# A hybrid transformer on one Trainium2 core: the decayed q and k operands of the decay attention stay in PSUM until their first rest is taken

## What is computed

```python
q = x @ W_q
k = x @ W_k
v = x @ W_v
latent_kv = (k + v) @ W_down_kv
k_rec = (latent_kv @ W_up_k)          # per head of 8
v_rec = (latent_kv @ W_up_v)
scores = einsum('bhqd,bhkd->bhqk', q, k_rec) / sqrt(d)
decay = exp(-0.01 * abs(t[:, None] - t[None, :]))
attn = softmax(scores * decay)
out = einsum('bhqk,bhkd->bhqd', attn, v_rec)
```

## Time and profile before

| | us |
|---|---|
| median of 3 runs | 1121.29 |
| lowest, highest | 1120.91, 1122.62 |
| profiled execution, its own time | 1125.32 |
| its span in the trace | 1123.5 |
| TensorE busy (share of the span) | 1041.1 (93%) |
| VectorE busy | 743.8 (66%) |
| ScalarE busy | 678.7 (60%) |
| GpSimd busy | 170.5 (15%) |

### The profile page before, as it was taken

How to read it: one execution, slowest core, us unless ns; L and a number is a source line. 1 busy time by engine, 2 the same in 40 slices (tenths; PEclk the granted TensorE clock), 3 DMA queues, 4 the chain that set the end, 5 groups by cost and what they waited for, 6 DMA issues and landing times.

```text
span 1123.5 us, 15969 instructions
## 1 busy us (share of the span) xinstructions
PE 1041.1 (93%) x6036; PEld 413.5 (37%) x6048; DVE 743.8 (66%) x1194; ACT 678.7 (60%) x1140; POOL 170.5 (15%) x119
## 2 busy tenths in 40 slices
PE   5799998988999999999999989999989988999998
PEld 2233333335433333333333334443333333334443
DVE  2787326348989999999999621126879898881110
ACT  4687525446078788888888774467556656634331
POOL 0222531006000000000000000000333342340000
PEclk9899999999989999999999999999989999999999
DMA  8000000038950321303000000000000000000000
GB/s 270 1 2 1 1 0 1 0 123 233 303 90 4 64 43 23 65 4 63 9 3 8 7 2 1 1 1 0 1 0 1 0 1 0 1 10 1 10 9 10
DMA packets 31203, 38.37 MB, mean 34 GB/s; under 512 B 7964, under 2 KB 22300, under 8 KB 30744
## 3 DMA queue, kind: packets, MB, share of 16 engines
q1 hardware_dynamic: 31128, 37.37, 13.2%
HBM read 23.23 MB, written 13.86 MB: 33 GB/s over the span
## 4 chain that ended last, share of the span: by engine, by line
PE 51%; DVE 23%; ACT 6%; issue 2%; another core or an unknown queue 1%; DVEq 0%; ACTq 0%
PE PS L1510 17%; DVE ffn L926 15%; PE PS L1038 6%; PE PS L1014 4%; DVE PS L1063 2%; PE PS L1495 2%; PE PS L1498 2%; PE PS L1521 2%; ACT arena L1048 2%; PE PS L1577 1%; PE PS L1080 1%; PE PS L1687 1%; PE PS L916 1%; DVE arena L1724 1%; PE PS L1677 1%
## 5 line engine op out<-in xcount | busy, mean ns | idle before, releaser
L1048 ACT ACTIVATE arena<-PS 128x384 f32<-128x384 f32 (+1 forms) x512 | 258.0, 547 | 84.4 <-PE PS L1014 72.9
L926 DVE CUSTOM_DVE_ANT_0 ffn<-PS,XP 128x1024 bf16<-128x1024 f32 x256 | 300.7, 1216 | 4.4 <-PE PS L916 4.4
L916 PE MATMUL PS<-arena 48*128 48x512 bf16 (+3 forms) x704 | 173.6, 325 | 5.6 <-DVE MX L926 5.5
L1014 PE MATMUL PS<-arena 50*128 50x512 bf16 (+3 forms) x640 | 169.4, 320 | 1.6 <-ACT arena L1048 1.3
L1038 PE MATMUL PS<-arena 128*32 128x256 f32 x2048 | 162.4, 393 | 1.0
L1540 ACT ACTIVATE arena<-PS,w_scl 128x512 f32<-128x512 f32 x64 | 43.5, 687 | 139.5 <-PE PS L1510 139.2
L1510 PE MATMUL PS<-arena,w_h2T 128*128 128x512 f32 x256 | 118.0, 607 | 0.0
L1510 PE MATMUL PS<-arena,w_h1T 128*128 128x512 f32 x256 | 115.3, 594 | 0.4 <-DVE arena L1549 0.4
L1014 PEld LDWEIGHTS PS<-arena 50*128 50x128 bf16 x640 | 50.4, 94 | 101.9 <-ACT arena L1048 70.2
L1724 DVE TENSOR_TENSOR_SCAN arena<-arena 128x512 f32<-128x512 f32 x64 | 81.4, 1273 | 0.3
L1510 PEld LDWEIGHTS PS<-arena,w_h2T 128*128 128x128 f32 x256 | 49.6, 195 | 61.1 <-issue 58.6
(11 more groups left out here) (228 smaller groups left out, 1558.0 us busy)
## 6 DMA issues: line engine op xcount, KB each, us to landing
arena<-scr SPq DMA_DIRECT2D x64, 192.0 KB, 5.7
scr<-arena SPq DMA_DIRECT2D x16, 384.0 KB, 5.5
scr<-arena SPq DMA_DIRECT2D x16, 256.0 KB, 4.9
scr<-arena SPq DMA_DIRECT2D x16, 128.0 KB, 3.3
XP<-xT SPq DMA_DIRECT2D x1, 1024.0 KB, 4.9
w_h1T<-h1T SPq DMA_DIRECT2D x1, 1024.0 KB, 6.7
w_h2T<-h2T SPq DMA_DIRECT2D x1, 1024.0 KB, 8.6
arena<-MH SPq DMA_DIRECT2D x64, 4.0 KB, 1.7
```

The lines of the kernel that those rows point to most:

```text
L916: mm = t.matmul(PS[:, bank, k0 - lo:k1 - lo], packed(m, g, v, slice(q * P, (q + 1) * P), KP), packed(m, g, 2 + v, slice(k0, k1), KP), star ...
L926: v.tensor_tensor_reduce(JUNK[:, u % 2, :], PS[:, bank:bank + 2, :].rearrange("p a b -> p (a b)"), STRIP[:, at:at + S], 1.0, -3.0e38, ALU. ...
L1014: mm = t.matmul(PS[:, score_bank(T, i), at:at + b_ - a_], packed(n, g, 2 + v, slice(kt * P, (kt + 1) * P), KP + MROWS), packed(n, g, v, sl ...
L1048: nc.scalar.activation(PT[:, T % 2, score_head(T, i), a0_:a1_], PS[:, score_bank(T, i), a0_:a1_], ACT.Exp).then_inc(s_free, 1)
```

## The change

The four decayed operands are no longer written to SBUF but to PSUM: operand 0 to bank 5, operand 1 back into bank 0, operand 2 to bank 6 and operand 3 back into bank 3. ScalarE casts the high piece from there, and VectorE's subtraction reads the operand from PSUM and the high piece from SBUF; only the first rest is written to `V32`. VectorE takes rests 0 and 1 ahead of the copy of v, and rests 2 and 3 behind it. The wait for the low piece of two chunks earlier moves from the multiplication to the subtraction, since that is now what overwrites `V32`. TensorE's projections of the next chunk wait for the first rests 0 and 1 of the chunk before (`a1_r1`, at 4c - 2), the rebuilt k for all four of them, and the attention's first unit for all sixteen.

```diff
@@ -761,13 +761,15 @@
             return T % 2 == 0
 
 
+        DECAYED = (5, 0, 6, 3)
+
         def a1_prep_pe(t):
             wait_loads(t, 3)
             for c in range(NCH):
                 x = XN[:, c * CH:(c + 1) * CH]
                 t.wait_ge(ln_free, ln_count(4, c))
                 if c > 0:
-                    t.wait_ge(a1_ver, 4 * c - 2)
+                    t.wait_ge(a1_r1, 4 * c - 2)
                 t.matmul(PS[:, 0, :], wqkv1[:, 0:P], x, start=True, stop=True)
                 t.matmul(PS[:, 1, :], wqkv1[:, P:2 * P], x, start=True, stop=False)
                 t.matmul(PS[:, 1, :], wqkv1[:, 2 * P:3 * P], x, start=False, stop=True).then_inc(a1_qkv, 1)
@@ -778,6 +780,8 @@
                 t.wait_ge(a1_latc, c + 1)
                 t.wait_ge(ln_free, ln_count(4, NCH - 1))
                 t.wait_ge(a1_v, c + 1)
+                if c > 0:
+                    t.wait_ge(a1_r1, 4 * c)
                 t.matmul(PS[:, 3, :], wlow[:, P:2 * P], LAT, start=True, stop=True)
                 for w in range(CH // P):
                     mm = t.matmul(PS[:, 4, w * P:(w + 1) * P], LAT[:, w * P:(w + 1) * P], wlow[:, 2 * P:3 * P],
@@ -802,7 +806,7 @@
                     a.wait_ge(a1_stored[c % 2], STORES)
                 for v in range(4):
                     a.wait_ge(a1_ver, 4 * c + v + 1)
-                    nc.scalar.copy(SPL[c % 2][:, v, 0, :], V32[c % 2][:, v, :]).then_inc(a1_hi, 1)
+                    nc.scalar.copy(SPL[c % 2][:, v, 0, :], PS[:, DECAYED[v], :]).then_inc(a1_hi, 1)
                 if c + 1 < NCH:
                     take_kv(c + 1)
                     take_latent(c + 1)
@@ -822,16 +826,21 @@
                     c = b * 2 + j
                     v.wait_ge(a1_qkv, c + 1)
                     for n, tab in ((0, FALL), (1, RISE), (2, RISE), (3, FALL)):
-                        v.wait_ge(a1_lo_free, 4 * c + n + 1)
                         if n == 2:
                             v.wait_ge(a1_kr, c + 1)
-                        v.scalar_tensor_tensor(out=V32[j][:, n, :], in0=PS[:, 0 if n < 2 else 3, :],
+                        v.scalar_tensor_tensor(out=PS[:, DECAYED[n], :], in0=PS[:, 0 if n < 2 else 3, :],
                                                scalar=SCALE if n < 2 else 1.0, in1=tab[:, j * CH:(j + 1) * CH],
                                                op0=ALU.mult, op1=ALU.mult).then_inc(a1_ver, 1)
+
+                    def rest(n):
+                        v.wait_ge(a1_hi, 4 * c + n + 1)
+                        v.wait_ge(a1_lo_free, 4 * c + n + 1)
+                        v.tensor_tensor(V32[j][:, n, :], PS[:, DECAYED[n], :], SPL[j][:, n, 0, :], ALU.subtract).then_inc(a1_r1, 1)
+                    rest(0)
+                    rest(1)
                     v.tensor_copy(XN[:, chunk(c)], PS[:, 4, :]).then_inc(a1_v, 1)
-                    for n in range(4):
-                        v.wait_ge(a1_hi, 4 * c + n + 1)
-                        v.tensor_tensor(V32[j][:, n, :], V32[j][:, n, :], SPL[j][:, n, 0, :], ALU.subtract).then_inc(a1_r1, 1)
+                    rest(2)
+                    rest(3)
 
         def a1_minus_ones(g):
 
@@ -1120,6 +1129,7 @@
             a1_prep_pe(t)
             idle_pe(t, 18, 7)
             t.wait_ge(a1_v, 1 + NCH)
+            t.wait_ge(a1_r1, 4 * NCH)
             for u in range(LEAD):
                 unit_pe(t, u, 0)
                 unit_pe(t, u, 1)
```

## The result

The changed kernel is slower. Its median over 8 runs is 1135.18 us (1131.75 to 1138.98), against 1122.3 us (1120.72 to 1128.14) for 8 runs of the kernel before; the medians lie 12.9 us apart. The ratio on record is 1.0096, 95% interval 1.0075 to 1.0116, which is 10.8 us, from 8.4 to 13.0. The profiled execution took 1135.8 us with a span of 1134.0, against 1125.32 and 1123.5: 10.5 us in either. The prediction had +10.1 us, and a median of 1131.4 in a range of 1128.0 to 1135.0.

A forecast was written before the change was run, and what follows sets the result against it. The prediction took a TensorE and ScalarE chain to bound the preparation, with VectorE off it. Three borders of 2.80 us (8.4) plus 1.7 for the clock gave +10.1 on 1121.3: 1131.4 us, range 1128.0 to 1135.0.

The forecast's parts named there:

- The path: Preparation: TensorE and ScalarE alone form the chain, 7.07 us a chunk; the new wait adds VectorE, 8.4 us over three borders.
- The term of 2.80 us a border: Next chunk's q projection: starts near 251.22 instead of 248.42, waiting for multiplications 2 and 3 and rests 0 and 1.
- Rests ready when VectorE reaches them: ScalarE's casts of the high pieces finish before rests 0 and 1 need them, margin 0.9 us; cost 0.
- Hidden parts: Rebuilt k's wait for rest 3, `packs(0)` moving at most 5.6 us, and VectorE's own end add nothing.
- Cost of PSUM operands: Multiplications writing PSUM and subtractions reading it: 0.4 us of VectorE time, under 0.1 us on the path.
- The gain of 3 to 4 us of VectorE time: Subtractions beside GpSimd's should always take about 0.69 us, saving 3 to 4 us of VectorE's busy time, worth 0.
- The clock: Idle gaps of about 2.7 us at borders trip TensorE's clock to 0.50 once, 1.7 us; bounds 0 to 5.2.
- rival C: Attention: the later start moves the clock dip at 312 to 319 us away, returning up to 1.4 us; 1128.3 us, chance 0.09.
- The sum: Whole kernel: 8.4 for the waits + 1.7 for the clock = 10.1 us slower, median 1131.4 us.

The follow-up runs named there:

- e1: The change with decayed operand 1 in bank 7, so the q projection waits for the first two multiplications as before: 1122.11 us, ratio 1.000 to the kernel before.
- e2: The kernel before, operands in SBUF, with rests 0 and 1 ahead of the copy of v and the new projection wait: 1140.57 us, ratio 1.0153.
- e5: The change with rests 0 and 1 ahead of multiplications 2 and 3 in VectorE's order: 1130.25 us, ratio 1.0081 to the kernel before.
- e4: The change with 9 instead of 18 idle matmuls behind the last chunk: 1132.94 us, ratio 1.0085 to the kernel before.
- e3: The change with five idle matmuls behind the rebuilt v of chunks 0 to 2: 1128.78 us, ratio 1.0055 to the kernel before.
- e7: The changed kernel itself run once more, for a second profile: 1131.11 us, ratio 1.0085 to the kernel before.
- e6: As e5, with ScalarE casting high pieces 0 and 1 of chunks 1 and 2 right behind their latent: 1123.93 us, ratio 1.0025 to the kernel before.

## Why the prediction was right, point by point

*The path.* That the chain of before never touches VectorE in this stretch, and that the new wait puts it in, was the right reading; e1 and e2 separate the wait from the memory. The term of 2.80 us a border was 0.1 us too small: 9.97 - 7.07 = 2.90 between the later borders. From the end of the rebuilt v to the projection it is 251.53 - 248.89 = 2.64 us, just the predicted figure, but by two errors that cancel: the multiplication starts 0.02 us behind the rebuilt v, put at 0.11, and TensorE starts 0.14 us behind rest 1, put at 0.05. What was too small is the lost overlap of one matmul with the next: the first projection holds the chain for 1.10 us where it held it for 0.86, 0.24 us instead of the 0.16 in the sum.

*Rests ready when VectorE reaches them.* Right: in the change VectorE waits for TensorE and never for a cast at this point. The theory of e5, that ScalarE is next once the order is turned, held.

*Hidden parts.* The rebuilt k's wait for rest 3, the DMA queue, VectorE's own end: none shows in the profile after. `packs(0)` went from 270.41 to 275.10, 4.7 us, under the 5.6 that were its bound, and did not bind in e4. The bound counted two borders; the 4.7 us are one border of 2.90, the low stretch of 1.49 and the 0.29 from before it.

*Cost of PSUM operands.* Put at under 0.1 us. The rests show none, 678 ns against 678; the multiplications into PSUM have a mean of 694 ns where those into SBUF had 681, which for the six on the path is 0.08 us. The gain of 3 to 4 us of VectorE time without a gain in time was right too. What the prediction did not see is that in the new order these would have been on the path: e2 shows that with both inputs in SBUF borders 2 and 3 hold TensorE 1.5 us longer each. Next to e2, the change pays for the same wait and gets a part of it back.

*The clock.* One low stretch of 1.7 us was taken from the row at 189 us; it was one, of 1.49 us, in either profile of the change, and e3 shows it to be the clock. The reason given for its being the first border was wrong, as e7 shows. The number of low stretches was luck in part: e2 had three, with longer gaps.

*Part of it comes back in the attention (rival C).* The dip of the clock that the kernel before has at 312 to 319 us did not move away with the later start: it shows from 322 us on in the first profile of the change and from 321 in the second. The attention was 0.2 us shorter in the first and 2.0 in the second. The second lacks a further low stretch, which stands at 663 to 668 us before and at 671 to 678 in the first. e1 lacks it as well, with its start only 0.45 us later than before, so its absence is not put down to the shift.

*The sum.* 8.4 + 1.7 = 10.1; measured from the profiles 10.46 at the first maximum and 10.5 at the end. The 10.46 are, to 0.02 us, 3 x 2.90 = 8.7 for the borders, 1.49 for the clock, and 0.29 us that lay ahead of the first border (its L787 starts at 247.98 against 247.69). So borders taken 0.3 us too small and a clock taken 0.2 us too large offset each other, and the rest is within what executions differ by. From the runs it is 10.8 (8.4 to 13.0), and in e7, on another chip than e1 to e4, 1.0085, 9.5 us. The median of the result, 1135.18, lies 3.8 us over the predicted one and 0.2 us over the upper end of the range. Of the 3.8 us, 1.0 is the base: 1121.29 was the median of three runs, and that of eight is 1122.3. The rest, 2.8 us, is what the medians differ by beyond the 10.1; with the ratio, 1121.29 x 1.0096 = 1132.1 us. Runs of one kernel differ by more than that (last section).

## What to carry to other kernels

Before a buffer is kept alive longer, look up who overwrites it next and on which engine's chain that writer stands: here one bank reused in place put VectorE's multiplications and subtractions between two TensorE stages that had met with no gap; another bank for the same operand (e1) took the loss away. A wait in a queue waits for all that stands ahead of the releasing instruction, so count that too. Busy time saved on an engine that the chain does not touch was worth nothing here (e1), and something only where the same edit put it on the chain (e2 against the change).

## What the runs showed of the hardware

A subtraction with both inputs in SBUF took up to 1676 ns while GpSimd subtracted beside it, and with one input in PSUM at most 681 ns in the same place, a median of 678 in both. The Trainium skill says (SBUF — State Buffer, section SBUF: two separate sides) that a VectorE operation with two SBUF inputs and a GpSimd operation that reads SBUF block one another for the whole instruction. The traces agree in both directions: with GpSimd at work beside them, two rests took 2.71 us in e2 and 1.28 us in the change.

Not expected was how much the spread of the times goes with the clock. The kernel before ran from 1119.32 to 1126.72 us in 21 runs; the three fastest had a mean granted clock of 0.988 to 0.991, the three slowest 0.979. From the first row maximum to the opening of the feed-forward, code that is the same in both, it is 412.7 us in the profile of before (278.15 to 690.81), 412.4 in that of the change (288.61 to 701.05), and 410.7 in its second (287.75 to 698.42); from there to the end of the span it is 432.7, 433.0 and 430.3 us.

```profile
287.75 1.23 DVE L935 CUSTOM_DVE_ANT_0 ffn<-PS,XP 128x1024 bf16<-128x1024 f32 x1 [4.04 <-PE PS L925]
```

The two profiles of the change are the same program with the same gaps. The mean granted clock was 0.980 in the first and 0.985 in the second, for spans of 1134.0 and 1128.7 us. One place where they part, 198 us behind the opening of the feed-forward, first in the first profile and then in the second:

```profile
899.00:903.00 4.00, 3.79 (x12) 1.13 (x12) 3.89 (x5) 2.21 (x3) 1.67 (x3) 0.58 0.01 2
```

```profile
896.00:900.00 4.00, 4.00 (x17) 1.49 (x16) 4.00 (x6) 2.60 (x5) 1.99 (x2) 1.00 0.01 2
```

The part behind the opening of the feed-forward is the same code in all nine profiles, and its length goes with the low clock in it, added up over windows of 1 us. It is 432.6 to 433.0 us with about 14 us of low clock (the kernel before, the change, e5), 431.8 with about 10 (e2, e6), and 430.3 to 430.4 with about 7 (e1, e3, e4, e7). So a dip costs here too, and how many of them there are differs between executions of one kernel. What fixes their place is open.
